# Re-timed side work in a software-pipelined decoder layer: bank reuse, layer-norm slots, GpSimd order and semaphore waits

## The chip, the cores and the metric

One core of a Trainium2 chip runs the whole kernel. The metric is the device time of one launch in microseconds. Five engines work in parallel, each through its own list of instructions in order: TensorE (PE), VectorE (DVE), ScalarE (ACT), GpSimd (POOL), and SyncE (SP), which here only issues DMAs. They meet through semaphores alone.

## The reference

Four sequences of 512 tokens, width 512, 16 heads of 32. All in fp32.

```
x = x + attn(LN(x))                      # causal self-attention, q/k/v/o projections with biases
x = x + causal_attn(LN(x), ctx, ctx)     # cross-attention, no projections
n = LN(x)
x = x + relu(n @ W_up.T) @ W_down.T + sum(softmax(top2(n @ W_gate.T))) * (n @ W_expert)
```

The projections run as three fp32r products of a high and a low half (hi*lo, lo*hi, hi*hi), so each projected tile is read out of PSUM twice: ACT writes the high half, DVE subtracts it to get the low half.

## The kernel before

**Steps and slots.** The work is a list of 64 pairs of heads: 32 pairs of self-attention (two pairs make a group G; 16 "own" groups) and 32 of cross-attention (16 "other" groups). `ORDER` puts the groups in sequence: 14 own, then other and own mixed, then other alone. Every engine walks the same loop over steps s = -4 to 74, each of 8 slots i; z = 8s + i numbers a slot. In step s PE computes the scores of pair s+1 (L466, one tile of 128 to 512 columns each slot) and turns (transposes) the probabilities of pair s (L480, 4 to 1 transposes a slot). In slot 0 of even steps it multiplies 32 probability tiles with the values (L513, the "pv" matmuls). DVE takes the negated maximum of each score tile (L680), ACT exponentiates it with a row sum (L908), POOL multiplies own probabilities by the reciprocal of the sum (`scaled`, L1021, four tiles per head), and ACT and DVE share the copies of turned tiles (L917, L690).

**Fills.** Into these slots a planner (`plan`, L136) puts the projections as "fills": Q, K, V, O, the transposes of the normalized x (L), and for each sequence f of the feed block FL (transposes of the normalized x, L534), FG (router gate, L583/L584), FU, FE and FD. Every fill gets one of two PSUM banks, m0 or m1, for its slots plus `held` slots. Turned tiles use the banks t0 and t1, and also m0 or m1 where these are free for long enough. `BEFORE` and `TURN_BEFORE` name the previous user of the bank, for whose readers PE waits. `empty` (L759 on DVE, L936 on ACT) reads a fill out in the slot in which it ends, and on DVE one slot later for Q, K and FL.

**Layer norms.** `ln_stats` and `ln_norm` (DVE, L707 and L735) run in the slots that `stats_slots` and `norm_slots` name, j = 1 to 3 for the self-attention of sequence j, j = 4 to 7 for the cross-attention of sequence j-4; `f_stats_of` and `f_norm` (L714, L743) do the same for the feed block. POOL makes the reciprocal root between them (`ln_scale` L1030, `f_scale` L1036).

**POOL's order within a step** (L1103 to L1137): `scaled(s, 1)`, `keys` (the high and low halves of the cross keys, L1054 and L1056), `scaled(s+1, 0)`, `added` (cross residual, L1064), `ln_scale`, `f_scale`, `biased` (residual plus output bias, L1045), at step 24 a memset of g_both (L1129), at step 32 the low half of the gate, and from step 38 on the splits of the feed weights (L1079, L1081).

**SP** loads the operands of the scores of pair P (`load_stack`, six DMAs of 128 KB) in step P-2, once their stack buffer is free, and the feed weights in turn through one buffer (V[1]), each once POOL has split the one before.

**Around the pv bank.** For an own group ACT and DVE read the high and low context out of it (`context_hi` L923, slot 2; `context_lo` L751, slot 5); for a cross group ACT copies it (`context_hi`, L934), PE transposes it back (`back`, L621, slot 4) and DVE scales it (`back_scaled`, L810).

## Time and profile before

| | |
|---|---|
| median of 3 runs | 721.66 us (721.66 to 722.08) |
| profiled execution, device time | 721.66 us |
| its span, first to last instruction | 719.6 us |
| mean granted TensorE clock | 0.99 |
| PE, DVE, ACT, POOL busy | 94%, 69%, 70%, 36% |

The device time holds 2.1 us around the span. In the profile a line such as `L480` is a line of the kernel. A row of the timeline gives start, duration, engine, what is written and read, the count, and in brackets how long the engine had been idle and who released it. The start of each score matmul (L466) on PE marks a slot, so the 512 of them tell which slot PE is in at any time: step 24 starts at 284.07 us, step 34 at 366.64, step 42 at 431.03, step 58 at 601.42.

### The profile page before, as it was taken

To read this page: it belongs to the slowest core of one execution; us is meant where nothing else is said; L and a number is where in the kernel's file an instruction comes from. 1 tells how busy PE (TensorE), PEld (TensorE's weight loads), DVE (VectorE), ACT (ScalarE), POOL (GpSimd) and SP (SyncE) were. 2 spreads that over 40 slices of the span, in tenths; PEclk is the share of its full clock that TensorE was granted. 3 is DMA by queue.
4 is the path that set the end of the run, shared out by engine and by line. 5 is a ranking of instruction groups with operands and counts; after the bars stand their busy time and mean duration, and the time that the engine had idled before them with its cause. 6 is when DMAs were issued, how large, how long until landed. Compare 5 with 4: busy or idle time off the path is not lost.

```text
span 719.6 us, 13877 instructions
## 1 busy us (share of the span) xinstructions
PE 677.8 (94%) x4488; PEld 523.9 (73%) x4488; DVE 498.8 (69%) x1730; ACT 501.0 (70%) x1450; POOL 257.8 (36%) x391
## 2 busy tenths in 40 slices
PE   7998999999999999999969987999989999899998
PEld 6776777767877677677756765777768777577786
DVE  6568666756766676767788789867887669564632
ACT  5678877767876677788899887676688657774110
POOL 3745545333555345751654424433211012000100
PEclk9999999999999999999999998999999999999999
DMA  9663433345433464355956685543363444510101
GB/s 316 171 156 77 125 82 89 75 115 146 117 77 89 117 178 117 84 123 132 273 123 166 158 232 120 148 109 96 88 174 91 113 99 104 141 45 1 58 1 58
DMA packets 52326, 86.12 MB, mean 120 GB/s; under 512 B 8608, under 2 KB 16800, under 8 KB 52256
## 3 DMA queue, kind: packets, MB, share of 16 engines
q1 hardware_dynamic: 52256, 85.25, 45.4%
q8 instruction: 36, 0.59, 0.4%
q14 instruction: 34, 0.28, 0.1%
HBM read 27.55 MB, written 7.34 MB: 48 GB/s over the span
## 4 chain that ended last, share of the span: by engine, by line
PE 77%; DVE 11%; ACT 6%; issue 2%; DMA 2%; POOL 1%; SPq 0%; ACTq 0%; POOLq 0%; DVEq 0%
PE t L480 15%; PE m L519 14%; PE m L520 13%; PE m L521 13%; PE pv L513 10%; PE s L466 8%; DVE probs L680 4%; ACT probs L908 3%; DVE prob L690 1%; DVE xT_lo L766 1%; ACT prob L917 1%; PE m L480 1%; DMA stack<-stage 1%; POOL probs L1021 1%; PE m L583 1%
## 5 line engine op out<-in xcount | busy, mean ns | idle before, releaser
L680 DVE CUSTOM_DVE_ANT_0 probs<-s,mask 128x128 f32<-128x128 f32 (+3 forms) x512 | 245.8, 482 | 135.2 <-PE s L466 132.9
L908 ACT ACTIVATE probs<-probs,negmax 128x128 f32<-128x128 f32 (+3 forms) x512 | 284.7, 559 | 44.6 <-DVE negmax L680 43.3
L480 PE MATMUL t<-ident,probs 128*128 128x128 f32 x1143 | 203.6, 276 | 12.1 <-ACT prob L917 5.0
L917 ACT ACTIVATE prob<-t 128x512 f32<-128x512 f32 (+1 forms) x232 | 125.3, 541 | 109.0 <-PE t L480 108.8
L466 PE MATMUL s<-stack 96*128 96x128 f32 (+3 forms) x512 | 197.5, 392 | 3.8 <-DMA stack<-stage 2.2
L1021 POOL TENSOR_SCALAR probs<-probs,rsum 128x128 f32<-128x128 f32 (+3 forms) x256 | 133.4, 539 | 181.8 <-DVE rsum L694 181.8
L480 PEld LDWEIGHTS t<-ident,probs 128*128 128x128 f32 x1143 | 144.6, 141 | 62.2 <-issue 7.8
L466 PEld LDWEIGHTS s<-stack 96*128 96x128 f32 x512 | 97.4, 190 | 16.5 <-DMA stack<-stage 3.0
L908 ACT ACTIVATION_READ_ACCUMULATOR probs<-probs,negmax 128x1 f32 x512 | 99.1, 194 | 0.0
L690 DVE COPY prob<-t 128x128 f32<-128x128 f32 (+1 forms) x217 | 76.7, 353 | 30.7 <-PE t L480 29.8
L519 PE MATMUL m<-xT_hi,w_lo 128*128 128x512 f32 x192 | 78.4, 409 | 0.9 <-DVE xT_lo L748 0.9
L520 PE MATMUL m<-xT_lo,w_hi 128*128 128x512 f32 x192 | 75.7, 394 | 0.0
L521 PE MATMUL m<-xT_hi,w_hi 128*128 128x512 f32 x192 | 75.5, 393 | 0.0
L519 PE MATMUL m<-w_hi,xT_lo 128*128 128x512 f32 x128 | 52.7, 412 | 0.0
L520 PE MATMUL m<-w_lo,xT_hi 128*128 128x512 f32 x128 | 50.4, 394 | 0.0
L521 PE MATMUL m<-w_hi,xT_hi 128*128 128x512 f32 x128 | 50.2, 392 | 0.0
L521 PEld LDWEIGHTS m<-xT_hi,w_hi 128*128 128x128 f32 x192 | 36.1, 188 | 8.6
L513 PE MATMUL pv<-prob,cv 128*32 128x128 f32 (+3 forms) x512 | 40.8, 463 | 1.6 <-ACT prob L917 1.4
L680 DVE DVE_READ_ACCUMULATOR2_ANT negmax<- 128x1 f32 x512 | 42.1, 82 | 0.0
L520 PEld LDWEIGHTS m<-xT_lo,w_hi 128*128 128x128 f32 x192 | 36.5, 190 | 2.8
L519 PEld LDWEIGHTS m<-xT_hi,w_lo 128*128 128x128 f32 x192 | 36.7, 191 | 2.5 <-DVE xT_lo L748 1.2
L513 PE MATMUL pv<-prob,V 128*32 128x128 f32 (+3 forms) x512 | 37.8, 435 | 0.0
(144 smaller groups left out, 955.0 us busy)
## 6 DMA issues: line engine op xcount, KB each, us to landing
stack<-stage SPq DMA_DIRECT2D x384, 128.0 KB, 2.3
xt<-in_x SPq DMA_DIRECT2D x16, 256.0 KB, 4.7
xres<-in_x SPq DMA_DIRECT2D x4, 1024.0 KB, 5.9
kraw<-in_ctxT SPq DMA_DIRECT2D x16, 256.0 KB, 3.1
cv<-in_ctx SPq DMA_DIRECT2D x16, 256.0 KB, 3.2
x<-xres SPq DMA_DIRECT2D x3, 1024.0 KB, 5.4
res<-x SPq DMA_DIRECT2D x8, 256.0 KB, 6.3
out<-res SPq DMA_DIRECT2D x2, 1024.0 KB, 4.8
```

Of the source, the lines that this page charges most:

```text
L466: nc.tensor.matmul(score_tile(P, i), stack[0:RS, P % 2, h, 0, chunk(qb)], stack[0:RS, P % 2, h, 1, 0:N], start=True, stop=True).then_inc(s ...
L480: mm = nc.tensor.transpose(dst[:, chunk(qb - kb)], probs[:, (2 * P + h) % 3, OFF[qb] + PART * kb:OFF[qb] + PART * kb + PART], ident[:, :])
L513: mm = nc.tensor.matmul(pv_bank[HD * j:HD * j + HD, PART * kb:T], v[:, HD * j:HD * j + HD], prob[kb][:, j, :], start=(kb == 0), stop=(kb = ...
L519: nc.tensor.matmul(dst, lhs[1], rhs[0], start=(c == 0), stop=False)
L520: nc.tensor.matmul(dst, lhs[0], rhs[1], start=False, stop=False)
L521: return nc.tensor.matmul(dst, lhs[0], rhs[0], start=False, stop=(c == KC - 1))
L583: nc.tensor.matmul(dst, g_both[:, c, :], xT_lo[:, c, :], start=(c == 0), stop=False)
L680: nc.vector.tensor_tensor_reduce(probs[:, (2 * P + h) % 3, OFF[qb]:OFF[qb + 1]], score_tile(P, i), mask[:, T - N:T], -SCALE, BIG, ALU.add, ...
L690: nc.vector.tensor_copy(prob[kb][:, 2 * (P % 2) + h, :], turned_tile(P, i)).then_inc(t_dve, 1)
L908: nc.scalar.activation(tile, tile, ACT.Exp, bias=negmax[:, P % 2, h, qb:qb + 1], scale=-1.0, accum_out=total).then_inc(p_exp, 1)
L917: nc.scalar.activation(prob[kb][:, 2 * (P % 2) + h, :], turned_tile(P, i), ACT.Copy).then_inc(t_act, 1)
L1021: nc.gpsimd.tensor_scalar(tile, tile, rsum[:, P % 2, h, qb:qb + 1], 0.0, ALU.mult, ALU.add).then_inc(p_done, 1)
```

## The change

Seven kinds of edit, in one patch:

- Q, K and FL no longer hold their bank for an extra slot; DVE still reads Q and K one slot late, but FL in the slot in which it ends. The planner's banks and predecessors shift with it.
- The statistics of j = 5 and j = 7 leave their two slots at the start of an even step for four slots spread over two steps; the norms of j = 5 to 7 and of the feed blocks go from two in each of two slots to one in each of four.
- In `turn`, PE waits once for all four scaled tiles of an own head, not for each tile before its transpose.
- ACT does `context_hi` after the exponential and the copy of slot 2; DVE does `context_lo` in slot 4.
- POOL does `scaled(s+1, 0)` as the last thing of a step, `added` before `keys`, and `ln_scale` one step later but for j = 6.
- SP loads the weight W_down one step earlier (43, not 44), and POOL splits it one step earlier.
- The loops that allowed two tiles in one slot are written with `index`.

```diff
--- before.py
+++ after.py
@@ -105,7 +105,7 @@
         return [z - 8, z - 7, z, z + 1]
     if j == B + 2:
         return [z + 24, z + 25, z + 28, z + 29]
-    return [z + 16, z + 16, z + 17, z + 17] if j == B + 1 else [z, z, z + 1, z + 1]
+    return [z + 1, z + 5, z + 9, z + 13] if j == B + 1 else [z - 7, z - 3, z + 1, z + 5]
 
 
 def norm_slots(j):
@@ -115,7 +115,9 @@
         return [z + 16, z + 17, z + 24, z + 25]
     if j == B:
         return [z + 2, z + 3, z + 5, z + 6]
-    return [z + 32, z + 32, z + 33, z + 33]
+    if j == B + 2:
+        return [z + 32, z + 33, z + 36, z + 37]
+    return [z + 28, z + 29, z + 32, z + 33]
 
 
 def f_stats_slots(f):
@@ -127,7 +129,7 @@
 def f_norm_slots(f):
 
     z = PAIRS * (PAIRS * (f + B + 1) + 2)
-    return [z, z, z + 1, z + 1]
+    return [z, z + 1, z + 2, z + 3]
 
 
 END = (feed_start(B - 1) + UNITS) // PAIRS + 1
@@ -141,8 +143,8 @@
         jobs.append((PAIRS * step + slot, slots, held, key))
 
     for n, G in enumerate(SELF_AT):
-        put(("Q", n), 2 * G - 4, 4 if n and n % KC == 0 else 0, 4, 1)
-        put(("K", n), 2 * G - 3, 0, 4, 1)
+        put(("Q", n), 2 * G - 4, 4 if n and n % KC == 0 else 0, 4)
+        put(("K", n), 2 * G - 3, 0, 4)
     for b in range(B):
         for t in range(NT):
             if b:
@@ -162,7 +164,7 @@
         put(("FG", f), 0, u + GATE_AT, 4, 3)
         for m in range(KC):
             if f < B - 1:
-                put(("FL", f, m), 0, u + 1 + 2 * m, 1, 1)
+                put(("FL", f, m), 0, u + 1 + 2 * m, 1)
             put(("FU", f, m), 0, u + UP_AT + 4 * m, 4)
             put(("FE", f, m), 0, u + EXP_AT + 4 * m, 4)
             put(("FD", f, m), 0, u + DOWN_AT + 4 * m, 4)
@@ -441,7 +443,7 @@
                     sp.wait_ge(o_mm, NT * B)
                     sp.wait_ge(x2_stored[2], 16)
                     load_x(res2, x2[2])
-                if s == SELF_END + 7:
+                if s == SELF_END + 6:
                     sp.wait_ge(f_lo_done, 2 * KC)
                     load_weight("downT", DOWN)
                 for f in range(B - 1):
@@ -469,14 +471,15 @@
             def turn(P, i):
 
                 h, kb = divmod(i, NT)
-                if kb == 0 and not own(P // 2):
-                    pe.wait_ge(p_exp, PAIRS * P + NT * (h + 1))
+                if kb == 0:
+                    if own(P // 2):
+                        pe.wait_ge(p_done, PAIRS * own_rank(P) + NT * (h + 1))
+                    else:
+                        pe.wait_ge(p_exp, PAIRS * P + NT * (h + 1))
                 if TURN_BEFORE[P, i] is not None:
                     pe.wait_ge(*emptied(TURN_BEFORE[P, i]))
                 dst = turned_tile(P, i)
                 for qb in range(kb, NT):
-                    if kb == 0 and own(P // 2):
-                        pe.wait_ge(p_done, PAIRS * own_rank(P) + NT * h + qb + 1)
                     mm = nc.tensor.transpose(dst[:, chunk(qb - kb)],
                                              probs[:, (2 * P + h) % 3, OFF[qb] + PART * kb:OFF[qb] + PART * kb + PART],
                                              ident[:, :])
@@ -866,12 +869,12 @@
                     if own((s + 1) // 2) and i == 5:
                         recip(s + 1, 0)
                     for key in ENDED.get(z - 1, ()):
-                        if key[0] in ("Q", "K", "FL"):
+                        if key[0] in ("Q", "K"):
                             empty(key)
                     for key in ENDED.get(z, ()):
-                        if key[0] not in ("V", "FG", "Q", "K", "FL"):
+                        if key[0] not in ("V", "FG", "Q", "K"):
                             empty(key)
-                    if s % 2 == 0 and own(s // 2 - 1) and i == 5:
+                    if s % 2 == 0 and own(s // 2 - 1) and i == 4:
                         context_lo(s // 2 - 1)
                     if s % 2 == 1 and other((s + 3) // 2) and i == 5:
                         query_lo((s + 3) // 2)
@@ -880,19 +883,15 @@
                     if s % 2 == 0 and other(s // 2 - 1) and i == (5 if s < NP else 4):
                         back_scaled(s // 2 - 1)
                     for j in range(1, 2 * B):
-                        for t in range(NT):
-                            if z == stats_slots(j)[t]:
-                                ln_stats(j, t)
-                        for t in range(NT):
-                            if z == norm_slots(j)[t]:
-                                ln_norm(j, t)
+                        if z in stats_slots(j):
+                            ln_stats(j, stats_slots(j).index(z))
+                        if z in norm_slots(j):
+                            ln_norm(j, norm_slots(j).index(z))
                     for f in range(B):
-                        for t in range(NT):
-                            if z == f_stats_slots(f)[t]:
-                                f_stats_of(f, t)
-                        for t in range(NT):
-                            if z == f_norm_slots(f)[t]:
-                                f_norm(f, t)
+                        if z in f_stats_slots(f):
+                            f_stats_of(f, f_stats_slots(f).index(z))
+                        if z in f_norm_slots(f):
+                            f_norm(f, f_norm_slots(f).index(z))
                         route(f, z - feed_start(f))
 
 
@@ -992,8 +991,6 @@
                         if s == step and i == NT:
                             for c in range(KC):
                                 split_hi(w, c)
-                    if s % 2 == 0 and 0 <= s // 2 - 1 < NG and i == 2:
-                        context_hi(s // 2 - 1)
                     P, k = divmod(z - 1 + PAIRS, PAIRS)
                     if other(P // 2) and own((s + 1) // 2):
                         exped(P, k)
@@ -1003,6 +1000,8 @@
                         turned(s, i)
                     if other(P // 2) and not own((s + 1) // 2):
                         exped(P, k)
+                    if s % 2 == 0 and 0 <= s // 2 - 1 < NG and i == 2:
+                        context_hi(s // 2 - 1)
                     if s % 2 == 1 and other((s + 3) // 2) and i == 3:
                         query_hi((s + 3) // 2)
                     for f in range(B):
@@ -1105,15 +1104,12 @@
                 if own(s // 2):
                     for qb in range(NT):
                         scaled(s, 1, qb)
+                if s % 2 == 1 and other((s - 3) // 2):
+                    added((s - 3) // 2)
                 if s % 2 == 0 and other(s // 2 + 2):
                     keys(s // 2 + 2)
-                if own((s + 1) // 2):
-                    for qb in range(NT):
-                        scaled(s + 1, 0, qb)
-                if s % 2 == 1 and other((s - 3) // 2):
-                    added((s - 3) // 2)
                 for j in range(1, 2 * B):
-                    if s == stats_slots(j)[-1] // PAIRS:
+                    if s == stats_slots(j)[-1] // PAIRS + (j != B + 2):
                         ln_scale(j)
                 for f in range(B):
                     if s == f_stats_slots(f)[-1] // PAIRS:
@@ -1133,8 +1129,11 @@
                         .then_inc(g_lo_done, 1)
                 for n, slot in enumerate((UP, EXPERT, DOWN)):
                     for c in range(KC):
-                        if s == SELF_END + 1 + ((0, 1, 1, 1), (4, 4, 5, 5), (8, 8, 9, 9))[n][c]:
+                        if s == SELF_END + 1 + ((0, 1, 1, 1), (4, 4, 5, 5), (7, 7, 8, 8))[n][c]:
                             f_split(n, slot, c)
+                if own((s + 1) // 2):
+                    for qb in range(NT):
+                        scaled(s + 1, 0, qb)
 
 
 def kernel(**inputs):
```

## Rows read from the trace of the kernel before

**Rows 1.** The page, part 1: engine, busy us (share of the span), x instructions.
```profile
PE 677.8 (94%) x4488; PEld 523.9 (73%) x4488; DVE 498.8 (69%) x1730; ACT 501.0 (70%) x1450; POOL 257.8 (36%) x391
```

**Rows 2.** Waits of the whole span: waiting <- releaser: us, times, longest.
```profile
POOL probs L1021 <- DVE rsum L694: 181.8, 60, 16.1
...
PE m L583 <- DVE xT_lo L766: 6.3, 4, 2.2
PE m L534 <- DVE xT_lo L766: 3.4, 6, 0.9
PE t L480 <- POOL probs L1021: 2.3, 8, 0.3
...
PE pv L621 <- ACT cn L934: 1.9, 4, 0.6
```

**Rows 3.** Timeline of step 24, POOL and PE: start us, us, engine, line, what.
```profile
288.03 2.30 POOL L1021 TENSOR_SCALAR probs<-probs,rsum 128x128 f32<-128x128 f32 x4 [2.94 <-DVE rsum L694]
...
292.43 2.39 POOL L1021 TENSOR_SCALAR probs<-probs,rsum 128x128 f32<-128x128 f32 x4
...
294.65 0.60 PE L480 MATMUL t<-ident,probs 128*128 128x128 f32 x4
...
294.79 1.28 POOL L1045 TENSOR_TENSOR xres<-xres,row 128x512 f32<-128x512 f32 x1
...
296.01 0.53 POOL L1129 MEMSET g_both<- 128x512 f32 x1
```

**Rows 4.** Timeline of slot 93, PE and DVE.
```profile
151.98 0.66 PE L534 MATMUL m<-ident,xt 128*128 128x128 f32 x4
152.34 0.72 DVE L775 SCALAR_TENSOR_TENSOR stage<-m,bias,stage 128x512 fp32r<-128x512 f32 x1
```

**Rows 5.** Timeline of slot 214, PE and DVE.
```profile
309.57 0.39 PE L480 MATMUL t<-ident,probs 128*128 128x128 f32 x2
...
310.05 0.75 DVE L775 SCALAR_TENSOR_TENSOR stage<-m,bias,stage 128x512 fp32r<-128x512 f32 x1 [0.27 <-ACT stage L952]
```

**Rows 6.** Groups by line: busy us, mean ns of one, idle us before.
```profile
L908 ACT ACTIVATE probs<-probs,negmax 128x128 f32<-128x128 f32 (+3 forms) x512 | 284.7, 559 | 44.6 <-DVE negmax L680 43.3
```

**Rows 7.** Timeline of steps 42 and 43, feed block 0, DVE and PE.
```profile
433.96 2.01 DVE L743 TENSOR_SCALAR f_xln<-xt,f_mv,f_rstd 128x512 f32<-128x512 f32 x2
...
436.84 1.98 DVE L743 TENSOR_SCALAR f_xln<-xt,f_mv,f_rstd 128x512 f32<-128x512 f32 x2
...
439.58 0.60 PE L534 MATMUL m<-ident,f_xln 128*128 128x128 f32 x4
...
448.82 0.67 PE L583 MATMUL m<-xT_lo,g_both 128*128 128x512 f32 x1 [2.18 <-DVE xT_lo L766]
```

**Rows 8.** Timeline of step 34's first two slots on DVE, first and last of eight.
```profile
369.79 0.69 DVE L707 BATCH_NORM_STATS2 stats<-res 128x6 f32<-128x512 f32 x1
...
373.48 0.18 DVE L709 BATCH_NORM_AGGREGATE mv<-stats 128x2 f32<-128x6 f32 x1
```

**Rows 9.** Stretches: window, length, busy us by engine, granted clock, DMA share, GB/s.
```profile
366.64:375.96 9.32, 7.27 (x67) 4.97 (x65) 8.52 (x33) 7.73 (x25) 8.36 (x12) 1.00 0.51 127
375.96:382.97 7.01, 5.29 (x34) 3.92 (x33) 5.80 (x24) 6.74 (x21) 6.74 (x13) 1.00 0.53 134
...
449.00:452.40 3.40, 3.40 (x13) 2.80 (x14) 2.14 (x6) 1.30 (x3) 0.00 (x0) 0.50 0.00 0
619.80:623.20 3.40, 3.40 (x22) 0.80 (x24) 0.00 (x0) 0.00 (x0) 0.00 (x0) 0.52 0.65 145
```

**Rows 10.** Timeline around step 45: DMA issue by SP, and PE's scores.
```profile
459.05 0.39 SPq L394 DMA_DIRECT2D V<-in_downT  x1
...
466.32 0.31 PE L466 MATMUL s<-stack 96*128 96x128 f32 x1
```

**Rows 11.** DMA issues: KB each, median us from issue to landing.
```profile
stack<-stage SPq DMA_DIRECT2D x384, 128.0 KB, 2.3
...
V<-in_downT SPq DMA_DIRECT2D x1, 1024.0 KB, 6.0
```

## The prediction

> **What bounds the kernel now.** I read the busy shares first. PE is busy for 677.8 us of 719.6 [rows 1], so 41.8 us of the span is PE idle, and nothing the patch does takes a matmul away: it can only shrink or grow that idle time, or push PE work into stretches at another clock. The waits come second [rows 2]. PE has no single large wait. It waits 6.3 us in 4 pieces for the router gate's operands (L583), 3.4 us in 6 for transposes of a normalized x (L534), 2.3 us in 8 for POOL's scaled tiles, 1.9 us in 4 for ACT's copy of the cross context. Third come stretches and timelines where these waits fall. The reader should see that PE's margin differs by stretch: through most of the self-attention it runs with no gap, so a stall put there is paid in full; in steps 34 and 35 ACT is busy for 14.47 of 16.33 us (7.73 of 9.32 and 6.74 of 7.01) [rows 9] and sets the pace, so there small PE stalls cost little and at most ACT's own 1.86 us idle can be won.
>
> The sum is made against the profiled execution, 721.66 us (span 719.6 and 2.1 around it), which equals the median of the runs shown.
>
> **POOL's order, step 24.** `scaled(25, 0)` now comes after everything else of the step. Nearly always that is harmless: POOL waits for the reciprocals 60 times, 3.0 us on average (181.8/60) [rows 2], and one residual or one rstd job of about 1.3 us fits in such a gap. `added` and `keys` never share a step with a problem: `added` runs at odd steps, where no `keys` runs. Step 24 is the exception, since it alone has `keys`, `biased` and the memset before a `scaled`. The first scaling ends at 290.33 (288.03 + 2.30), `keys` fills the time to 292.43, and only then does `scaled(25, 0)` take 2.39 us; PE turns those tiles at 294.65 [rows 3], with the last one just done. In the new order 1.28 + 0.53 us come first: the scaling starts at 294.24 and ends at 296.63, so the turn is late by 296.63 - 294.65 = 2.0 us. The work behind it, PE's next scores, waits too, since PE is in order. Some small gaps behind it close: **+1.8**, bounds 0 and 2.0. At step 34 the same edit sets an rstd before `scaled(35, 0)`; I count that with the statistics below.
>
> **One wait for four tiles.** It matters only where POOL is late: the 8 waits come as 4 pairs [rows 2]. There three transposes that ran beside POOL now run after it. One adds 0.1 us (four take 0.60, two 0.39) [rows 3, 5], so 0.33 us a place, 1.3 in all. Three of the four lie where ACT sets the pace: **+0.7**, bounds 0 and 1.3.
>
> **No held slot for Q and K.** DVE reads Q and K one slot late either way, so a bank is now handed out in the very slot in which DVE empties it. Following the planner, eight users get such a predecessor. Two are L tiles (slots 93 and 157): before, L in slot 93 waited for an O tile that DVE had finished, and ran at 151.98, while K's low half ended at 152.34 + 0.72 = 153.06 [rows 4]. Now it waits for K: 1.08 us late, twice. Half of it comes back, because PE waits for such tiles anyway, 0.6 us at a time over the span (3.4/6) [rows 2]: +1.3 of 2.2. Six are turned tiles (slots 22, 190, 214, 222, 246, 254). At 22 and 246 PE waits as long for ACT already, at 190 K is out in time. At 214 the turn ran at 309.57, and the wait for Q stood one turn later, released at 310.05 + 0.75 = 310.80 [rows 5]; now PE stops 1.2 us earlier, and one score and two transposes (some 0.2 us each) move behind the wait: 0.4 to 0.45 each at 214, 222 and 254, 1.2 in all; at the worst DVE's next maximum is late by the full 1.2 at each. **+2.5**, bounds 0 and 4.7 (2.2 + 2.5, every stall in full but for what PE already waits).
>
> **ACT's context after the exponential.** Of the 16 cross groups only 4 have PE waiting for the copy [rows 2]; behind one more exponential (559 ns on average, and some 0.1 until the next starts) [rows 6] the copy is up to 0.75 us later there, 3.0 in all. But that exponential is then earlier, and its turned tile is what PE waits for next: **+0.8**, bounds 0 and 3.0. The low half of the own context, moved a slot up on DVE, has ACT's copy ready in all but two groups: 0.
>
> **Feed blocks: norms spread, FL read a slot earlier.** In block 0 DVE used the pv matmuls' time for two norms (2.01 us) and the next slot for two more (1.98), and PE's first FL ran at 439.58, 0.8 us after the last [rows 7]. With one norm a slot the fourth stands behind two more maxima and copies; FL is late by 1.5 to 2 us, and DVE, full through here, has about 1 us of work more in the way. Reading FL one slot earlier takes one maximum of 512 columns and one copy (about 1.1 us) out of the way of the low half that releases the gate at 448.82 after 2.18 us idle [rows 7]. The two cancel in block 0 and nearly in block 1, whose norms are as close to its FL. Blocks 2 and 3 have four more slots between: block 2 gains 1.0, block 3 runs with no maxima and gains nothing. Net -0.5. The 3.4 us at 0.52 of the clock behind block 2's gate wait [rows 9] cost about 1.6 us; with an even chance that the shorter wait spares them: -0.8. **-1.3**, bounds -9.8 (below) and +3.5 (the first FL of blocks 0 and 1 late and nothing back).
>
> **The statistics of j = 5.** Four of them hold DVE from 369.79 to 373.66 [rows 8], in a stretch where ACT then runs short of maxima. Spread over steps 32 and 33 they find DVE half idle. ACT has 1.86 us to win; the rstd of 1.3 us that POOL does between two scalings moves before them: **-1.4**, bounds -1.9 and 0. Statistics and norms of j = 6 and 7 move in stretches where PE has no gap: 0; if that cover went they would cost what one norm takes, under 1 us.
>
> **SP.** In step 43 SP now waits for POOL to split W_expert before it goes on. That is done at 459.05, where W_down was issued; behind it now stand the six stack DMAs of pair 46 and what follows. PE needs the first half at 466.32 [rows 10]. With 2.3 us of landing it would be there by about 464; the weight lands at 459.05 + 6.0 = 465.05 [rows 11], and a stack behind it at up to 467.3. **+0.3**, bounds 0 and 1.0.
> The Trainium skill (DMA: Bandwidth & Descriptors, section Queues, rings and completion order) says that descriptors are consumed in ring order on each DMA engine. By that rule the stack can't pass the weight and lands after 465.05, so the stall would be near the 1.0; by landing time alone it is 0. The sum takes neither.
>
> **Sum.** 1.8 + 0.7 + 2.5 + 0.8 - 1.3 - 1.4 + 0.3 = +3.4: 725.1 us, slower by 0.5%.
>
> **Rivals.** *Faster through the gate.* Place: the PE waits at FG and FL of blocks 0 to 2. If what holds FG is only the order on DVE, reading FL earlier ends 5.1 us of gate waits (6.3 less block 3's 1.2) and 1.7 of FL waits [rows 2], and with them both stretches of 3.4 us at half clock [rows 9], 3.0 us: 9.8 saved. 721.66 + 4.7 - 9.8 + 0 = 716.6, with 4.7 the other terms (3.4 + 1.3). It decides from 6.1 us saved on (4.7 + 1.44). For it: the gate's idle ends in every block with that low half. Against it: the norms put nearly the same work before it.
> *Nothing.* The stalls fall into idle time that PE has anyway, and gains and losses of 1 to 3 us cancel: 721.7. For it: 41.8 us idle. Against it: at 93, 157 and 294 PE is without gap.
> *Slower by more.* The longer stalls before FL in blocks 0 and 1 and behind W_down bring further stretches at half clock, 1.7 us each (3.4 at 0.5) [rows 9], and SP's delay passes to the next pair: 725.1 + 2 x 1.7 + 2 = 730.5. For it: idle of about 2 us came ahead of the stretch at 449 [rows 7, 9]. Against it: of the four gate waits, only two have such a stretch behind them.
>
> **How the numbers follow.** Within 0.2% (1.44 us) is what a measurement of this kernel can't tell from no change. Forecast 0.50, slower by more 0.10, nothing 0.20, faster 0.20. So slower 0.60, same 0.20, faster 0.20. The likeliest case alone runs from 723.1 to 729. The range goes to 719.0, leaving out the better half of the faster case (about 0.1), and to 731.0, leaving out part of the worse (under 0.1).
>
> **What would show it.** POOL's scaling around 294 should start after a residual and a memset, and PE's turn should come 2 us later after the start of its step. L534 in slots 93 and 157 should show about 1 us idle released by L775. The waits of L583 should stay near 6 us, with block 2's smaller, and the waits of L534 should grow for blocks 0 and 1. L621 should wait more than 1.9 us. ACT should be nearly full in steps 34 and 35, which should be shorter by over 1 us. The first scores of pair 46 may wait for a DMA. The prediction is wrong if the gate waits fall by over 4 us, if the stalls at 93, 157 and 294 appear but the following steps take their time back, or if steps 32 to 35 are longer.

## The result, and the profile after

| | before | changed |
|---|---|---|
| median of 4 runs each (lowest to highest) | 721.66 us (718.62 to 722.08) | 730.98 us (729.90 to 731.96) |
| ratio, 95% interval | | 1.0148 [1.0121, 1.0175] |
| profiled execution, device time (span) | 721.66 (719.6) | 730.95 (729.1) |

The patch makes the kernel slower by 9.3 us. The forecast was 725.1, slower by 3.4, with a range up to 731.0. (The ratio is not the quotient of these two medians: it rests on more runs, 15 of the changed kernel. In the rounds of experiments below the kernel before took 720.5 to 720.7 us in the median of 11 to 25 runs, so the cost is nearer to 10 us. The steps below are compared in the two profiled executions, which are 9.3 us apart.) The busy times of the changed kernel's page, against [rows 1]:

```profile
PE 678.7 (93%) x4488; PEld 526.2 (72%) x4488; DVE 503.4 (69%) x1730; ACT 504.1 (69%) x1450; POOL 258.9 (36%) x391
```

PE is busy 0.9 us more and the span is 9.5 us longer: nearly all of it is idle time. The waits of the changed kernel (waiting <- releaser: us, times, longest) say for whom, against [rows 2]. The names of lines moved by 2 or 3: L480 is now L483, L583 is L586, L621 is L624, L534 is L537.

```profile
PE m L586 <- DVE xT_lo L769: 5.2, 4, 1.8
PE m L483 <- POOL probs L1020: 4.6, 2, 3.0
PE m L483 <- DVE stage L778: 4.4, 5, 1.2
PE s L468 <- DMA stack<-stage: 4.3, 3, 2.4
PE pv L624 <- ACT cn L933: 4.3, 4, 1.1
...
PE m L537 <- DVE stage L778: 2.8, 3, 1.3
PE t L483 <- POOL probs L1020: 2.6, 2, 1.5
```

The gate's wait fell only from 6.3 to 5.2 us. Waits for POOL's scaled tiles grew from 2.3 us in 8 short pieces to 7.2 us in 4 long ones, one of them 3.0 us. The waits for DVE's `stage` come to 7.2 us in 8, where before had 1.2 in 3 (L775), and those for the stack to 4.3, where before had 2.2.

A busy share has no places, so I cut both traces into steps, by the start of each step's first score matmul on PE. "Changed" is the length less that of the same step before:

| steps | changed, us | what stands there |
|---|---|---|
| up to step 0 | -1.2 | a stretch at half clock that before had at 8.7 us is absent |
| 11, 19 | +0.96, +0.95 | L in slots 93 and 157 |
| 24, 27 | +0.33, +0.38 | one wait for four tiles |
| 25 | +1.68 | POOL's late `scaled(25, 0)` |
| 26, 31 | +0.46, +0.59 | turned tiles behind Q |
| 28, 40 | +0.54, +0.49 | ACT's context |
| 32, 33 | +1.36, -1.24 | an exchange between the two; ACT's context alone gives +1.35 and -1.35 |
| 34, 35, 36 | +0.39, +2.69, +0.80 | root of j = 5 before `scaled(35, 0)`; its norms; half clock |
| 41, 42, 43 | +0.17, +1.13, -2.27 | feed block 0 |
| 44 | +2.68 | W_down |
| 50, 51 | +2.14, -1.55 | feed block 1; half clock from 536.9 us on |
| 60 | -2.00 | feed block 2; the stretch of before at 619.7 is absent |

Steps 34 to 36 and 44 are the surprise. The changed kernel's POOL through steps 34 and 35 (start, us, engine, line, what, in brackets the idle time before and who ended it):

```profile
377.05 2.06 POOL L1020 TENSOR_SCALAR probs<-probs,rsum 128x128 f32<-128x128 f32 x4 [3.09 <-DMA stack<-stage]
379.06 0.61 POOL L1053 CAST stage<-kraw 128x512 fp32r<-128x512 f32 x1
379.75 1.27 POOL L1055 TENSOR_TENSOR stage<-kraw,stage 128x512 fp32r<-128x512 f32 x1
381.00 0.23 POOL L1031 TENSOR_SCALAR veps<-mv 128x4 f32<-128x4 f32 x1
381.32 1.04 POOL L1033 TENSOR_TENSOR rstd<-veps,neg_half 128x4 f32<-128x4 f32 x1
382.35 2.07 POOL L1020 TENSOR_SCALAR probs<-probs,rsum 128x128 f32<-128x128 f32 x4
```

DVE's reciprocal for that last job was there at 380.94:

```profile
380.77 0.17 DVE L697 RECIPROCAL rsum<-rowsum 128x4 f32<-128x4 f32 x1
```

`keys` ends 0.08 us after it and would have cost nothing. The root then takes 1.35 us, and only behind it does the scaling start. PE turns the head the moment the fourth tile is done:

```profile
379.17 0.66 PE L483 MATMUL m<-ident,probs 128*128 128x128 f32 x4 [1.63 <-POOL probs L1020]
...
384.47 1.11 PE L483 MATMUL m<-ident,probs 128*128 128x128 f32 x4 [2.96 <-POOL probs L1020]
```

The transposes take 1.11 us and not 0.66, because the granted clock has fallen to its lower level. Stretches of the changed kernel (window, length, busy us of PE, PEld, DVE, ACT, POOL, granted clock, DMA share, GB/s):

```profile
371.50:381.21 9.71, 6.76 (x66) 4.67 (x65) 6.67 (x28) 8.75 (x27) 6.14 (x11) 1.00 0.63 151
381.21:390.91 9.70, 6.75 (x34) 6.28 (x33) 5.92 (x24) 6.51 (x19) 7.50 (x13) 0.65 0.27 68
383.50:386.90 3.40, 2.43 (x12) 2.43 (x13) 0.52 (x3) 1.31 (x5) 1.36 (x4) 0.50 0.52 136
386.90:390.30 3.40, 3.40 (x17) 3.14 (x16) 2.65 (x10) 2.70 (x10) 3.40 (x5) 0.52 0.00 0
```

Step 35 (second row) took 7.01 us before [rows 9]. Two stretches of 3.4 us at 1.2 GHz follow one another, the first beginning inside PE's wait. ACT, which I had taken for the bound here, is busy for 6.51 us of 9.70.

At step 44 PE waits for an operand of its scores. PE and SP of the changed kernel, then its DMA issues from 468 to 473 us (KB each, median us to landing):

```profile
468.35 0.39 SPq L396 DMA_DIRECT2D V<-in_downT  x1
468.84 3.97 SPq L381 DMA_DIRECT2D stack<-stage  x6
...
477.18 0.33 PE L468 MATMUL s<-stack 96*128 96x128 f32 x1 [2.44 <-DMA stack<-stage]
```

```profile
V<-in_downT SPq DMA_DIRECT2D x1, 1024.0 KB, 7.1
stack<-stage SPq DMA_DIRECT2D x6, 128.0 KB, 6.4
```

The weight lands at about 468.35 + 7.1 = 475.45, and the stack 1.7 us behind it, though it was issued right behind it and takes 2.3 us over the whole span [rows 11].

### The profile page after: what moved, and what is told of

It reads as the page before. It is cut to its first block, busy times and chain, and to the rows that moved or that the text cites. A ratio compares the mean times of both kernels' runs of the same rounds, so it can differ in the third digit from the quotient of the medians.

```text
span 729.1 us, 13877 instructions
## 1 busy us (share of the span) xinstructions
PE 678.7 (93%) x4488; PEld 526.2 (72%) x4488; DVE 503.4 (69%) x1730; ACT 504.1 (69%) x1450; POOL 258.9 (36%) x391
## 4 chain that ended last, share of the span: by engine, by line
PE 76%; DVE 9%; ACT 5%; DMA 4%; POOL 3%; issue 2%; SPq 2%; POOLq 0%; DVEq 0%; ACTq 0%
PE t L483 14%; PE m L522 14%; PE m L523 13%; PE m L524 13%; PE pv L516 9%; PE s L468 8%; DMA stack<-stage 3%; DVE probs L683 3%; ACT probs L907 2%; PE m L483 2%; DVE xT_lo L769 1%; SPq L381 1%; DVE prob L693 1%; POOL probs L1020 1%; ACT prob L916 1%
## 5 line engine op out<-in xcount | busy, mean ns | idle before, releaser
L483 PE MATMUL t<-ident,probs 128*128 128x128 f32 x1100 | 196.4, 277 | 5.0 <-POOL probs L1020 2.6
L916 ACT ACTIVATE prob<-t 128x384 f32<-128x384 f32 (+1 forms) x225 | 120.8, 537 | 105.3 <-PE t L483 105.2
L483 PEld LDWEIGHTS t<-ident,probs 128*128 128x128 f32 x1100 | 140.0, 142 | 50.8 <-issue 6.1
L483 PE MATMUL m<-ident,probs 128*128 128x128 f32 x180 | 33.5, 291 | 10.2 <-POOL probs L1020 4.6
```

The costliest lines, as they stand in the source:

```text
L483: mm = nc.tensor.transpose(dst[:, chunk(qb - kb)], probs[:, (2 * P + h) % 3, OFF[qb] + PART * kb:OFF[qb] + PART * kb + PART], ident[:, :])
L916: nc.scalar.activation(prob[kb][:, 2 * (P % 2) + h, :], turned_tile(P, i), ACT.Copy).then_inc(t_act, 1)
```

## The experiments

Unless an entry says otherwise, each kernel is the kernel before with one part of the patch. Ratios are to the kernel before, with 95% intervals. A half-clock stretch is worth up to 1.7 us and falls at other places from kernel to kernel, so that a median alone can't carry a term of 1 us; step lengths can.

**The parts alone, first round.** POOL's order:

```diff
+added                        # before keys
 keys
-scaled(s + 1, 0, qb)
-added
-if s == stats_slots(j)[-1] // PAIRS:
+if s == stats_slots(j)[-1] // PAIRS + (j != B + 2):
...
+scaled(s + 1, 0, qb)         # last of the step
```

> The kernel before, with POOL's new order alone (scaled(s+1, 0) last in a step, added before keys, ln_scale a step later). Theory 1: the order is what costs most, through the two steps where more than one POOL job stands before a scaling: step 24 (residual 1.3 us and memset 0.5 us) longer with 25 by 1.5 to 2.0 us, and steps 34 and 35 by 1 to 1.5 us for the rstd, perhaps 1.7 us more where the stall brings a stretch at half clock: 724.5 to 727. Theory 2 (the moved statistics and norms cost the time of steps 32 to 36): only step 24 shows, 723.5.

Measured: 721.03 us, 0.9997 [0.998, 1.0015]. Step 25 is 1.68 longer, as forecast; step 35 is 0.13 shorter. Alone this order moves the root of j = 5 into step 35, where it does no harm. Only with the spread statistics does it return to step 34.

One wait for four tiles:

```diff
-pe.wait_ge(p_done, PAIRS * own_rank(P) + NT * h + qb + 1)   # per tile
+pe.wait_ge(p_done, PAIRS * own_rank(P) + NT * (h + 1))      # once
```

> The kernel before, with one wait for all four scaled tiles alone. Theory 1: it costs 0.3 us at each of the four places where POOL is late, 1.3 us at most, and nothing elsewhere: 722 to 723. Theory 2 (the single waits were what let PE run on in steps 34 and 35): 2 us or more in steps 34 and 35: 724.

Measured: 722.36 us, 1.0026 [1.0007, 1.0046]. Steps 24 and 27 are 0.31 and 0.32 longer. In steps 34 and 35 PE now stands in one piece:

```profile
373.87 0.66 PE L481 MATMUL t<-ident,probs 128*128 128x128 f32 x4 [1.62 <-POOL probs L1022]
378.02 1.06 PE L481 MATMUL t<-ident,probs 128*128 128x128 f32 x4 [1.81 <-POOL probs L1022]
```

Those steps are 0.26 and 0.76 longer. A half-clock stretch (378 to 382) lies in the second. In the kernel that has POOL's order as well (below) the clock is full in both, and they are 0.26 and 0.27 longer. So the one wait costs 1.2 us at all its places together, as the first theory has it.

The new slots of statistics and norms:

```diff
-return [z + 16, z + 16, z + 17, z + 17] if j == B + 1 else [z, z, z + 1, z + 1]
+return [z + 1, z + 5, z + 9, z + 13] if j == B + 1 else [z - 7, z - 3, z + 1, z + 5]
...
-return [z + 32, z + 32, z + 33, z + 33]
+if j == B + 2:
+    return [z + 32, z + 33, z + 36, z + 37]
+return [z + 28, z + 29, z + 32, z + 33]
```

> The kernel before, with the statistics of j = 5 and 7 and the norms of j = 5 to 7 and of the feed blocks in their new slots alone. Theory 1: steps 32 to 36 get no longer and may win up to 1.5 us, since the burst of 3.9 us on DVE is gone; steps 42 and 50, where the first transpose of the feed block waits for the fourth norm, each get 1 to 2 us longer and give part back: 721 to 723.5. Theory 2: steps 32 to 36 get 3 to 4 us longer: 725.

Measured: 724.14 us, 1.0049 [1.0026, 1.0071]. Steps 34 to 36 are longer by 0.88 + 0.42 + 1.12 = 2.42, not shorter. Step 42 is 1.74 longer and step 43 is 2.17 shorter. The granted clock is full in steps 34 to 36 of this kernel. Steps 35 and 36, and the two norms of j = 5 that now stand in slots 284 and 285, beside POOL's work:

```profile
378.45:385.88 7.43, 5.43 (x34) 3.93 (x33) 6.39 (x24) 6.68 (x21) 6.26 (x11) 1.00 0.35 88
385.88:394.69 8.81, 7.03 (x61) 4.28 (x61) 8.16 (x28) 6.04 (x20) 1.28 (x1) 1.00 0.67 163
```

```profile
383.98 1.42 DVE L737 TENSOR_SCALAR V<-res,mv,rstd 128x512 f32<-128x512 f32 x1
386.26 1.25 DVE L737 TENSOR_SCALAR V<-res,mv,rstd 128x512 f32<-128x512 f32 x1
```

The kernel before did all four under the pv matmuls of step 36, where POOL had nothing to do, in 1.00 us a pair:

```profile
384.96 1.00 DVE L735 TENSOR_SCALAR V<-res,mv,rstd 128x512 f32<-128x512 f32 x2
386.77 1.00 DVE L735 TENSOR_SCALAR V<-res,mv,rstd 128x512 f32<-128x512 f32 x2
```

FL read in the slot in which it ends, not held:

```diff
-put(("FL", f, m), 0, u + 1 + 2 * m, 1, 1)
+put(("FL", f, m), 0, u + 1 + 2 * m, 1)
-if key[0] in ("Q", "K", "FL"):
+if key[0] in ("Q", "K"):
```

> The kernel before, with FL read one slot earlier and not held alone. Theory 1: this is the one part that saves: the gate waits of blocks 0, 1 and 2 each get about 1 us shorter, so steps 43, 51 and 60 are shorter by 1 to 2 us each, and the stretches at half clock behind blocks 0 and 2 may go: 717 to 719. Theory 2 (DVE is so full that the order does not matter): 721 to 722.

Measured: 718.29 us, 0.9961 [0.9939, 0.9983], the one part that wins. Its gate waits, as PE's waits have them:

```profile
PE m L583 <- DVE xT_lo L766: 5.2, 4, 1.8
```

So 1.1 us less than [rows 2]; a read one slot earlier does not end this wait. More comes from the clock: step 60 is 1.98 shorter, because the stretch of [rows 9] at 619.8 is not there. The same part of this kernel's span:

```profile
612.00:625.00 13.00, 11.56 (x89) 8.52 (x90) 8.52 (x29) 10.03 (x31) 0.92 (x1) 1.00 0.43 102
```

Over the profiles of all kernels: ten do not read FL earlier, and each has a half-clock stretch that begins between 618.8 and 627.5; seven read it earlier, and none has one there. The gate wait of block 2 is 1.19 or 1.20 us in all seven, and 1.57 before.

**The parts alone, second round.** Q and K not held (`put(("Q", n), ..., 4, 1)` to `..., 4)`, K likewise):

> The kernel before, with no held slot for Q and K alone. Theory 1: steps 11 and 19 are 0.95 us longer each, nothing of it given back, because PE now stands at L until DVE has read K; with the turned tiles of steps 26, 27 and 31 some 1.2 us more: 724.5 to 725. Theory 2 (half of the L stalls is given back within the step): 1 us for the two L sites, 723.5.

Measured: 724.99 us, 1.0046 [1.0025, 1.0066]. Steps 11 and 19 are 0.95 and 0.94 longer, each behind a stall such as this one:

```profile
153.51 0.66 PE L534 MATMUL m<-ident,xt 128*128 128x128 f32 x4 [1.25 <-DVE stage L775]
```

Steps 26 and 31 add 0.45 each, step 27 0.24. W_down a step earlier (`SELF_END + 7` to `+ 6`, splits `(8, 8, 9, 9)` to `(7, 7, 8, 8)`):

> The kernel before, with W_down loaded and split a step earlier alone. Theory 1: the stack of pair 46 lands behind the 1 MB weight, PE waits 2 to 2.5 us for it at the start of step 45: 724. Theory 2: in the changed kernel the wait came of the earlier shifts, and here it is under 1 us: 722.5.

Measured: 721.48 us, 1.0012 [0.9993, 1.003]; but step 44 is 2.36 longer, behind

```profile
464.68 0.33 PE L466 MATMUL s<-stack 96*128 96x128 f32 x1 [1.56 <-DMA stack<-stage]
```

and steps 42 and 43 are 2.85 shorter, where half-clock stretches of before are absent. The median hid the cost. The stall is 1.56 us here and 2.44 in the changed kernel; it depends on how long before PE's scores the weight is issued, 7.3 us here and 6.4 there.

ACT's context behind the exponential:

```diff
-context_hi(s // 2 - 1)        # first of slot 2
 exped(P, k); turned(s, i)
+context_hi(s // 2 - 1)        # after both
-if s % 2 == 0 and own(s // 2 - 1) and i == 5:
+if s % 2 == 0 and own(s // 2 - 1) and i == 4:
```

> The kernel before, with ACT's context_hi after the exponential and DVE's context_lo a slot earlier alone. Theory 1: the four waits for the cross context grow from 0.6 and 0.4 us to 1.1 us, 2.3 us in all, of which the earlier exponentials give back most; steps 32 and 33 shift against each other: 721.5 to 723. Theory 2 (nothing given back): 724.

Measured: 722.66 us, 1.0021 [1.0002, 1.0041]. Steps 28 and 40 are 0.54 and 0.49 longer, and the wait for ACT's copy grew from 1.9 [rows 2] to 4.5 us:

```profile
PE pv L621 <- ACT cn L934: 4.5, 5, 1.1
```

One of the five is new, 0.90 us in step 34, ahead of 6.8 us at half clock; that step is 1.33 longer. The changed kernel has only four (4.3 us) and no such wait there.

**Which combination makes steps 34 to 36.** POOL's order and the one wait together:

> The kernel before, with POOL's new order and the one wait. Theory 1: the two are additive but for the 0.3 us a place, and together with the statistics they make the 3.9 us of steps 34 to 36: 725 to 728, steps 34 to 36 longer by 1.5 to 4 us. Theory 2: as the order alone, within 0.5 us.

Measured: 723.53 us, 1.0042 [1.0004, 1.008]; steps 34 to 36 only 0.53 longer, at full clock. With the new slots as well:

> The kernel before, with POOL's new order, the one wait and the new slots together. Theory 1: it is their combination that costs the 3.9 us of steps 34 to 36. Only with both the new slots (statistics of j = 5 done in step 33) and the new order does the rstd of 1.3 us stand before scaled(35, 0), and PE then stands at the one wait for near 3 us: steps 34 to 36 longer by 3.5 to 4.5 us, 728. Theory 2 (the parts add): steps 34 to 36 longer by 2.4 + 0.5 = 2.9 us, 727; and the planner's banks for the turned tiles make up the rest in the changed kernel.

Measured: 727.74 us, 1.0094 [1.0071, 1.0116]. Steps 34 to 36: 0.51 + 2.28 + 1.11 = 3.90, against 3.88 in the changed kernel, with the same stall:

```profile
381.64 1.08 PE L483 MATMUL t<-ident,probs 128*128 128x128 f32 x4 [2.95 <-POOL probs L1024]
```

The statistics of j = 5 spread, and nothing else (the first line of the slots' diff, j = 5 alone):

> The kernel before, with the four statistics of j = 5 alone spread over steps 32 and 33. Theory 1: POOL, which now does rstd and two residuals (3.8 us) between scaled(34, 0) and scaled(34, 1), is 1 us late, and step 34 gets 0.9 us longer; steps 35 and 36 do not: 722.5. Theory 2 (what helps DVE helps ACT): steps 34 and 35 get 1 us shorter.

Measured: 720.29 us, 0.9975 [0.9955, 0.9995]. Steps 34 and 35 of this kernel, which answer to [rows 9]:

```profile
367.17:377.38 10.21, 7.39 (x67) 4.78 (x65) 6.68 (x28) 8.98 (x28) 9.53 (x14) 1.00 0.58 142
377.38:384.15 6.77, 5.19 (x34) 3.94 (x33) 5.36 (x23) 6.02 (x18) 5.61 (x11) 1.00 0.38 97
```

DVE fell from 14.32 to 12.04 us, and the two steps are 0.65 us longer, not shorter. The loss is in step 34 (0.89), as the first theory has it: POOL's root now stands ahead of the scaling of the second head, which starts at 373.54, 0.8 us after its reciprocal (372.74). With all the new slots it was 2.42 us, so 0.66 more in step 35 and 1.12 in step 36 go with the norms of j = 5, the only other job that moved there. The median gain lies elsewhere: steps 42 and 43 are 2.86 shorter, as in the kernel with W_down early, where stretches of before are absent.

FL early, with the four statistics of j = 5 under the pv matmuls (`[z, z, z + 1, z + 1]`):

> The kernel before with FL read one slot earlier, and the statistics of j = 5 in slots 256 and 257 (under the pv matmuls of step 32, where neither DVE nor POOL has anything that PE waits for, with their rstd in step 32). Theory 1 (in steps 34 and 35 the loop through POOL, PE, DVE and ACT sets the pace, and both the burst and the rstd stand in it): 1 to 2 us under FL alone, 716 to 717. Theory 2 (ACT alone sets the pace there): as FL alone, 718.

Measured: 718.41 us, 0.9963 [0.9942, 0.9984], no better than FL alone. Its steps 34 and 35 do test the forecast gain without the root in the way, at full clock: DVE is busy for 11.29 us instead of 14.32, and they are 0.30 us shorter (16.03 against 16.33).

**Undoing parts in the changed kernel.** The root of j = 5 one step later:

```diff
-if s == stats_slots(j)[-1] // PAIRS + (j != B + 2):
+if s == stats_slots(j)[-1] // PAIRS + (j != B + 2) + (j == B + 1):
...
+if j == B + 1:
+    return [z + 32, z + 33, z + 34, z + 35]    # its norms
```

> The changed kernel with the rstd of j = 5 one step later (step 35, behind no scaling that PE waits for) and its norms in slots 288 to 291. Theory 1 (that rstd before scaled(35, 0) and the clock stretches behind the stall are what steps 34 to 36 pay): these steps get 2 to 3 us shorter than in the changed kernel, the stall of 3.0 us at the turn of pair 35 falls to under 1.8 us: 728 to 729. Theory 2 (DVE's norms in slots 284 and 285 are what hurt): the same total, but the stall of 3.0 us stays. Theory 3 (bank order): no change, 731.

Measured: 727.78 us, 1.0088 [1.0062, 1.0113], 3.2 below the changed kernel. The run moves two things, the root and the norms of j = 5, which leave step 35. Step 35 is 7.09 us, as before, and the turns of steps 34 and 35 wait 1.6 us each:

```profile
378.80 0.66 PE L485 MATMUL m<-ident,probs 128*128 128x128 f32 x4 [1.62 <-POOL probs L1022]
382.78 0.66 PE L485 MATMUL m<-ident,probs 128*128 128x128 f32 x4 [1.63 <-POOL probs L1022]
```

A half-clock stretch now lies in step 37, which is 1.38 longer, so that steps 34 to 37 get back only 1.5 us in this profile. Another 1.7 us come from step 44, which this edit does not touch: SP issues W_down 8.2 us before PE's scores instead of 6.4, and the stall is 0.70 us instead of 2.44.

W_down back in step 44 (the two numbers above, undone):

> The changed kernel with W_down loaded in step 44 and split in steps 45 and 46 again, nothing else undone. The changed kernel took 730.98 us, 9.3 over the kernel before. Theory 1 (the stall of 2.44 us before the first scores of pair 46 is a cost of its own, since the stack's DMAs land behind the 1 MB weight): step 44 shorter by 2.4 to 2.7 us than in the changed kernel, no wait of PE for a DMA of the stack there, 728.3 us, ratio to the kernel before 1.009. Theory 2 (the stall only moves: PE waits as long for FL's or FU's operands behind it): within 0.7 us of the changed kernel, 731, ratio 1.013. In both, stretches at half clock may fall elsewhere, 1.7 us each, so the step lengths decide.

Measured: 728.87 us, 1.0118 [1.0097, 1.0138]. Step 44 has its old length to 0.05 us, 2.7 less than in the changed kernel; the first theory held. The six issues of the same stack (window 461 to 466) now go out ahead of the weight and land in 2.3 us, not 6.4:

```profile
stack<-stage SPq DMA_DIRECT2D x6, 128.0 KB, 2.3
```

Q and K held again:

> The changed kernel with the held slot of Q and K given back, nothing else undone; FL stays a slot earlier and not held. Theory 1 (the terms add up: L in slots 93 and 157 waits 1.25 us each for DVE, the turned tiles a little): steps 11 and 19 shorter by 0.95 us each, steps 26 and 31 by some 0.5 each, together 3.0 us: 728.0 us, ratio 1.0087. Theory 2 (in the changed kernel the later waits of steps 24 to 37 swallow this stall, so that giving it back wins only at 11 and 19): 1.9 us: 729.1, ratio 1.010.

Measured: 731.15 us, 1.0125 [1.0098, 1.0152], with two of six runs at 727.2 and 727.6 and the others at 731.0 to 731.6. Steps 11, 19, 26 and 31 lose 0.96, 0.95, 0.46 and 0.46, so 2.8 us as the first theory has it, and steps 34 to 36 keep their 3.75. But the profiled execution (731.59) has two stretches at half clock that the changed kernel does not have:

```profile
25.50:28.90 3.40, 3.40 (x11) 2.77 (x12) 2.65 (x9) 1.10 (x4) 0.59 (x1) 0.57 0.81 187
476.70:480.10 3.40, 3.40 (x12) 2.76 (x12) 2.18 (x6) 1.05 (x2) 1.77 (x2) 0.53 1.06 213
```

Each begins within 0.7 us behind a wait of PE for a stack that is longer than in the changed kernel: 2.54 us up to 25.35 (1.04 there) and 2.89 us up to 476.39 (2.44 there). Step 0 starts 2.4 us later than in the changed kernel and step 45 is 1.6 longer, 4.0 together. The stall at L is gone and the median is the same; that four of six runs fell so is not explained.

All three back:

> The changed kernel with three things put back at once: the held slot of Q and K; W_down in step 44; and the reciprocal root of j = 5 on POOL in step 35, its norms in slots 288 to 291. Theory 1 (terms add): 730.98 less 3.0 (held) less 2.4 (W_down) less 3.2 (root of j = 5, as measured against the changed kernel) = 722.4, ratio 1.001; the wait of step 25 (+1.7) and ACT's context (+1.0) are left, and the feed blocks give 2 to 3 back. Theory 2 (the three costs overlap, since PE's later waits take up what an earlier one leaves): 725 or more, ratio 1.005 or above.

Measured: 724.50 us, 1.0051 [1.0032, 1.0069], so 6.5 of the 9.3 us are recovered. The three taken by their own steps would give 2.8 + 2.7 + 2.9 = 8.4. The profiled executions are 5.4 apart (730.95 and 725.59), 3.0 short of that. One stretch at half clock that the changed kernel has not (at 70 us, step 4) costs 1.7, the start 0.4 and steps 42 and 43 1.6, while steps 50 and 51 give 0.7; these are places that the three edits do not touch. The clock is full in steps 34 to 37; steps 34 to 36 are 1.10 longer than before, and step 44 is unchanged.

## Why the prediction was right in direction and wrong in size

Term by term, from the step lengths, with the run that shows each:

| term | forecast | measured | shown by |
|---|---|---|---|
| POOL's order, step 24 | +1.8 | +1.7 | that part alone |
| one wait | +0.7 | +0.7 (24, 27); +0.5 more in 34, 35 | that part alone; with POOL's order |
| no held slot | +2.5 | +2.8 | alone, and undone |
| ACT's context | +0.8 | +1.0 (28, 40) | that part alone |
| feed blocks, clock in them | -1.3 | -2.4 | block 2: FL alone |
| statistics, root and norms of j = 5 | **-1.4** | **+3.9**, the 0.5 above in it | root and norms undone; the three parts together |
| SP, W_down | **+0.3** | **+2.7** | alone, and undone |
| before step 0 | 0 | -1.2 | a stretch that is absent |

The measured column sums to 9.2 (with the 0.5 counted once), the traces differ by 9.3 in device time.

**The failed step** is the one that reads "the rstd of 1.3 us that POOL does between two scalings moves before them: -1.4". It failed in three ways.

The gain was wrong. I took ACT's 1.86 us of idle in steps 34 and 35 as something a lighter DVE could win back. In the kernel with only those statistics spread, DVE is lighter by 2.3 us and nothing is won, though there POOL's root stands in the way; with both out of these steps (FL early, statistics under the pv matmuls) DVE is lighter by 3.0 us and 0.3 are won. That ACT "sets the pace" there, since it is busy most of the time, did not hold. My reading, argued from the order of the work and not from a run, is that ACT's gaps lie where its next maximum waits for PE's scores, these stand behind PE's turn, and the turn waits for POOL; a chain round four engines, in which a stall in any of them is paid.

The place was wrong. For the root I had only asked whether POOL has the time in sum. It has: POOL is busy for 13.64 of 19.41 us. But in step 34 the keys alone already fill the gap up to the reciprocal, to within 0.08 us. The root behind them has no cover, and 1.35 us go straight to PE. It is the same counting that I did for step 24 and did not do for step 34, although the prediction named it as the same edit. On top, the one wait turns three short waits of PE into a single one of 2.96 us, against 1.63 with the root out of the way: 1.3 us for the root.

The norms of j = 5 had no term at all. The prediction priced those of j = 6 and 7 (at 0) and passed over these, two of which go from under the pv matmuls of step 36 to slots 284 and 285, beside POOL's work. At full clock the new slots cost 1.8 us more than the spread statistics alone (2.42 less 0.65).

The clock is the smaller part. The granted clock of the changed kernel is at half for 6.8 us from 383.5 on, and for 3.4 us in two kernels with the same stall, the three parts together and Q and K held again; these lose as much in steps 34 to 36, 3.90 and 3.76 against 3.88. A single stretch of 3.4 us in step 35 costs 0.4 us with FL alone and 0.5 with the one wait (against the same wait at full clock). No run has the root in its new place at full clock, so how the 3.9 divides is an estimate: undoing root and norms at full clock gives 2.8 back (3.88 less 1.10), of which 1.3 is the root's stall and 0.6 the norms in step 36 (1.14 with Q and K held again, 0.54 with all three back), and some 0.9 is left for the clock and the norms in step 35. The prediction had itself named longer steps 32 to 35 as a sign of being wrong; they are 3.2 us longer.

**The one wait** came out at 0.7 only because its other places, steps 34 and 35, are counted with j = 5. I had discounted them since "ACT sets the pace" there; they cost as much as the rest, 1.2 us together, near the bound of 1.3.

**SP's term** was of the right mechanism and mis-sized, outside its bound of 1.0. I had put the weight's issue at 459.05, 7.3 us ahead of the scores [rows 10]. In the changed kernel it is issued at 468.35, 6.4 ahead of the 474.74 at which PE was ready: 0.9 lost. The weight took 7.1 us and not 6.0 [rows 11]: 1.1 more. The stack landed 1.7 behind it, 0.6 sooner than I allowed for: 1.0 + 0.9 + 1.1 - 0.6 = 2.4, the stall. The Trainium skill (DMA: Bandwidth & Descriptors, section Queues, rings and completion order) has descriptors consumed in ring order on each engine. The trace agrees: the six small transfers right behind the weight take 6.4 us in the median, and 2.3 in the kernel where they go out ahead of it. The prediction weighed both readings and took a value nearer to the wrong one. From the weight's issue to PE's first use of the stack it is 8.8 to 9.3 us in all four kernels that stall here (6.4 + 2.44, 6.4 + 2.89, 8.2 + 0.70, 7.3 + 1.56), so the stall is the part of this that the weight's lead over PE's scores does not cover.

**The feed blocks** were better than forecast by 1.1. Block 0 has a new wait of 1.39 us for its first FL and a gate wait of 1.81:

```profile
450.55 0.63 PE L537 MATMUL m<-ident,f_xln 128*128 128x128 f32 x4 [1.39 <-DVE f_xln L746]
...
458.63 0.50 PE L586 MATMUL m<-xT_lo,g_both 128*128 128x512 f32 x1 [1.81 <-DVE xT_lo L769]
```

The first costs 1.4 and the second gives back 0.4 (from 2.18), so they do not cancel, though I had said that they would. That the block is 1.0 shorter all the same (steps 41 to 43) goes with the clock: two stretches before, at 431.9 and 449.0, and one now, at 441.4. In the two kernels with the root of j = 5 later, which have two there as well, steps 42 and 43 together are 0.5 longer than before. Block 1 is 0.6 longer, with a stretch at 536.9 that before had not; in the three kernels made from the changed one that lack it, steps 50 and 51 together come to -0.1. So the two blocks give 0.4, where the working had them lose 0.5, and that is luck with the clock. Block 2 gives 2.0 against 1.8 (1.0 and the half of 1.6): its wait is only 0.37 shorter, and the rest is the spared stretch, to which I gave an even chance.

**The held slot, POOL's step 24 and the context** came out to 0.3 us each, by counting single instructions against single rows. L in slot 93 stands as forecast:

```profile
152.02 0.66 PE L537 MATMUL m<-ident,xt 128*128 128x128 f32 x4 [1.25 <-DVE stage L778]
```

and so does the turn of step 25, in the changed kernel 297.41 - 294.90 = 2.5 us into its step, against 0.9 before [rows 3]:

```profile
294.63 0.52 POOL L1125 MEMSET g_both<- 128x512 f32 x1
295.14 2.22 POOL L1020 TENSOR_SCALAR probs<-probs,rsum 128x128 f32<-128x128 f32 x4
...
297.41 0.66 PE L483 MATMUL t<-ident,probs 128*128 128x128 f32 x4 [1.46 <-POOL probs L1020]
```

**The rivals.** "Slower by more", 730.5, came nearest in number and in mechanism, W_down's delay, but not in the clock: it put two further stretches behind FL, and there is about one more in all (18.1 us at half clock against 14.6), with 6.8 us of it behind the stall for POOL. "Faster through the gate" holds for FL alone, at 2.5 to 3 us instead of 9.8. "Nothing" fell.

## What to carry to other kernels

Where a loop runs round several in-order engines, do not call the one with the highest busy share the bound: look at the row behind each hand-over and ask what would end it a microsecond earlier or later. An order of work on a side engine has to be counted at each step where it meets the handed-over tile, since the one job too many is found there and not in the sum. A large transfer put in front of small ones delays them by its own landing time, so count from its issue to the first reader of what is queued behind it. When work moves off a busy place, look at what runs beside it in the new one: four norms took 2.00 us where POOL was idle, and two took 2.67 beside POOL.

## What the runs showed of the hardware

Stretches at a granted clock of 0.50, 3.4 or 6.9 us long, occur one to six times in a profile, and their places change from kernel to kernel. Over all 17 profiles, each one that begins before 700 us does so inside an idle of PE of 0.5 to 3.0 us or at most 1.9 us behind its end. Not every such idle has one behind it: the changed kernel waits 1.81 us for the gate of block 0 (up to 458.63) and keeps its clock. The price differs too: 0.4 us in step 35 with FL alone, 1.7 in step 4 of two kernels. Medians of kernels that differ by 1 to 3 us can therefore hide or contradict their own step lengths: W_down early costs 2.4 us in step 44 with a median ratio of 1.0012, and the spread statistics cost 0.65 in steps 34 and 35 with one of 0.9975.

The norm on DVE that took about 1.0 us in [rows 7] took between 0.53 and 1.37 us in block 0 of the changed kernel, one instruction at a time:

```profile
447.77 1.37 DVE L746 TENSOR_SCALAR f_xln<-xt,f_mv,f_rstd 128x512 f32<-128x512 f32 x1
...
449.87 0.53 DVE L746 TENSOR_SCALAR f_xln<-xt,f_mv,f_rstd 128x512 f32<-128x512 f32 x1
```

The traces show what goes with it. The 17 profiles hold 816 norms of this form. The 434 that have no POOL instruction beside them take 0.45 to 0.55 us each; all that take longer, up to 1.65, overlap one. Some that overlap take 0.45 as well, so it is not every POOL instruction, and no run separates which.
